# Banded attention with routed experts on one core: small tiles first, norms over more quads, the last stage's loads begun in the experts' block

## The reference

```python
xn = (x - mu) * rsqrt(var + EPS) * ln_gamma + ln_beta
abel_out = gelu(xn @ abel_w + abel_b)
topw, topi = top_k(xn @ moe_gate_w + moe_gate_b, 2); topw = softmax(topw)
h = gelu(einsum('bsd,edh->ebsh', xn, ew1) + eb1)          # 8 experts
moe_out = sum over the two chosen of (h @ ew2 + eb2) * topw
for i in range(3): moe_out = moe_out @ expm(gens[i])
gate = sigmoid(concat(abel_out, moe_out) @ gc_w + gc_b)
return x + abel_out * (1 - gate) + moe_out * gate
```

## Time and profile before

| | us |
|---|---|
| median of three timed runs | 1724.65 (1723.74 to 1725.66) |
| the profiled execution | 1724.25 |
| its span in the trace | 1722.4 |
| PE busy | 1500.2 (87%) |
| DVE busy | 1219.9 (71%) |
| ACT busy | 891.6 (52%) |
| POOL busy | 686.2 (40%) |
| DMA | 241.23 MB, 140 GB/s in the mean |

### The profile page before, as it was taken

One profiled execution on the slowest core, in us unless ns is written; L12 is line 12 of the kernel. 1 busy time (PEld: TensorE's weight loads), 2 busy tenths in 40 slices (PEclk: granted clock), 3 DMA queues, 4 the chain that ended last, 5 costly groups with the idle time before them and its releaser, 6 DMA issues. The chain is left out here.

```text
span 1722.4 us, 33082 instructions
## 1 busy us (share of the span) xinstructions
PE 1500.2 (87%) x10271; PEld 1033.1 (60%) x10272; DVE 1219.9 (71%) x3678; ACT 891.6 (52%) x1775; POOL 686.2 (40%) x698
## 2 busy tenths in 40 slices
PE   7999999999989999998999898799999999999300
PEld 5755455555545555554555466688888888888200
DVE  5667788888788788878977855456556555566197
ACT  3146766776676677667667664233333333332144
POOL 1011233533443343344244415144444444445277
PEclk9999999999999999999999999899999999999755
DMA  8132244345435434543543347655656565655397
GB/s 219 58 123 69 86 156 148 120 141 173 128 106 179 156 114 137 173 131 111 173 155 111 114 148 240 188 100 117 141 103 149 105 151 103 153 105 102 64 329 222
DMA packets 184174, 241.23 MB, mean 140 GB/s; under 512 B 23464, under 2 KB 154672, under 8 KB 183920
## 3 DMA queue, kind: packets, MB, share of 16 engines
q1 hardware_dynamic: 158464, 204.49, 37.4%
q0 software_dynamic: 25584, 35.15, 12.1%
HBM read 132.21 MB, written 104.72 MB: 138 GB/s over the span
## 5 line engine op out<-in xcount | busy, mean ns | idle before, releaser
L1116 ACT ACTIVATE pexp<-scT 128x512 f32<-128x512 f32 x768 | 436.4, 598 | 244.3 <-PE scT L882 241.9
L1322 DVE TENSOR_REDUCE mx<-work 128x1 f32<-128x320 f32 (+2 forms) x1024 | 500.3, 546 | 53.0 <-PE work L859 52.3
L1931 POOL DMA_INDIRECT y_rows<-rows_add,row_of x135 | 215.4, 1596 | 288.1 <-DMA y_rows<-rows_add,row_of 200.3
L882 PE MATMUL scT<-w 128*128 128x192 bf16 (+3 forms) x1536 | 281.1, 275 | 27.2 <-ACT pexp L1116 22.6
L859 PE MATMUL work<-w 126*128 126x320 bf16 (+4 forms) x1280 | 267.7, 295 | 25.8 <-DVE mx L1322 20.2
L1964 PE MATMUL h_ps<-inT,w1c 128*128 128x256 f32 (+1 forms) x1136 | 248.8, 373 | 4.6 <-DVE inT L2018 2.4
L1977 PE MATMUL o_ps<-w,hT 128*128 x1080 | 246.5, 381 | 5.8 <-ACT hT L1897 5.8
L1905 ACT ACTIVATE rows_add<-rows_out,row_share 128x257 f32<-128x257 f32 x135 | 61.8, 503 | 345.8 <-DVE rows_out L2036 243.9
L1964 PEld LDWEIGHTS h_ps<-inT,w1c 128*128 128x128 f32 x1136 | 210.5, 193 | 33.1 <-issue 3.1
L882 PEld LDWEIGHTS scT<-w 128*128 128x128 bf16 x1536 | 123.3, 97 | 176.3 <-ACT pexp L1116 116.3
L1977 PEld LDWEIGHTS o_ps<-w,hT 128*128 128x128 f32 x1080 | 200.3, 191 | 31.3 <-issue 6.9
(11 more groups left out here) (220 smaller groups left out, 2061.1 us busy)
## 6 DMA issues: line engine op xcount, KB each, us to landing
w<-split_spill SPq DMA_DIRECT2D x384, 128.0 KB, 2.8
split_spill<-split SPq DMA_DIRECT2D x64, 384.0 KB, 3.0
rows_in<-z_rows SPq DMA_DIRECT2D x64, 265.0 KB, 4.8
y_rows<-pre SPq DMA_DIRECT2D x16, 514.0 KB, 5.6
y<-y_rows SPq DMA_DIRECT2D x16, 514.0 KB, 6.6
x_rows<-x SPq DMA_DIRECT2D x16, 512.0 KB, 2.7
abel_rows<-pre SPq DMA_DIRECT2D x16, 512.0 KB, 3.6
abel_in<-abel_rows SPq DMA_DIRECT2D x16, 512.0 KB, 4.5
```

Source lines behind the costliest of these rows:

```text
L882: ins = nc.tensor.matmul(scT[n % 2][:, at:at + hi - lo], tile(kst[par][0:K_EXP, h, :], t), qst[par][0:K_EXP, h, lo:hi], start=True, stop=True)
L1116: nc.scalar.activation(pexp[:, (q * GROUP + n) % NPB, :], scT[n % 2][:, :], ACT.Exp, scale=DH ** -0.5).then_inc(s_exp, 1)
L1322: emptied(nc.vector.reduce_max(mx[:, c:c + 1], bank(s, "max", b, h, t)[:, 0:n], AX_X), s, "max", b, h, t)
L1931: pool.indirect_dma_start(kept.y_rows, bass.IndirectOffsetOnAxis(ap=row_of[n][:, r:r + 1], axis=0), rows_add[n % 2][:, r, :], None, comput ...
```

## The change

Four things change. (1) The eight norms of a step are done at units n = 1 and 3 of two quads each: norm_ctx in quads 4 and 5 (3 and 4 in step 16), norm_x in quads 6 and 7. (2) The order of places: place 0 has the number of the last pair (two blocks, the one that can be taken over), places 1 to 7 are the singles, places 8 to 70 are the other pairs; `tiles` writes out 12 tiles ahead of the loop instead of 4. (3) The last stage's y and base buffers are laid into w2 and w1 (5 of y, 8 of base) by the class `Tail`; SP loads base of batches 0 to 7 inside the experts' block as soon as the last w1 copy is done, and y of batches 0 to 3 when all adds have landed. (4) In the last stage a store waits only for the tile it takes; the sums of the last batch go from POOL to VectorE; a first sigmoid is done ahead of its inputs.

```diff
-LAST_NORM_CTX, LAST_STATS_AT, LAST_Z_AT = 3, 6, 10
+LAST_NORM_CTX, LAST_STATS_AT, LAST_Z_AT = (3, 4), 6, 10
-NORM_CTX, NORM_X = 5, 6
+NORM_CTX, NORM_X = (4, 5), (6, 7)
...
-    wide = np.concatenate([np.arange(NE), np.arange(NE) * region, np.arange(pairs), pairs + k // 2,
-                           np.zeros(pairs), k % 2 * P, spare]).astype(np.float32)
+    wide = np.concatenate([np.arange(NE), np.arange(NE) * region, [pairs - 1], pairs + k // 2, np.arange(pairs - 1),
+                           [0], k % 2 * P, np.zeros(pairs - 1), spare]).astype(np.float32)
...
+        self.ODDS_AT = 0
...
-                        if q == (LAST_NORM_CTX if s == B else NORM_CTX) and finish:
-                            norm_ctx(s - 2, n)
-                        if q == NORM_X and (not isinstance(s, int) or s + 1 < B):
-                            norm_x(s + 1, 1 - par, n)
+                        at = LAST_NORM_CTX if s == B else NORM_CTX
+                        if q in at and finish and n % 2:
+                            norm_ctx(s - 2, 2 * at.index(q) + n // 2)
+                        if q in NORM_X and s + 1 < B and n % 2:
+                            norm_x(s + 1, 1 - par, 2 * NORM_X.index(q) + n // 2)
...
-            no, before_last, behind = kept.pair_no, NE - 1, slice(z.PAIRS - 1, z.RTILES)
+            no, before_last, behind = kept.pair_no, NE - 1, slice(z.ODDS_AT, z.ODDS_AT + NE)
...
+class Tail:
...
+        self.YB, self.BB, self.BSEMS, self.AHEAD = 5, NE, 4, 4
...
+        self.base = [w1[:, n, :, :].rearrange("p k f -> p (k f)").rearrange("p (j d) -> p j d", d=z.D)
+                     for n in range(self.BB)]
+        self.y = [flat2[:, n * yw:(n + 1) * yw].rearrange("p (j w) -> p j w", w=z.YW) for n in range(self.YB)]
...
+    def load_base(self, sp, kept, z, b):
+        landed = self.f_early if b < self.BB else self.f_bs[b % self.BSEMS]
+        sp.dma_start(self.base[b % self.BB], kept.of_batches(kept.base_rows, z)[b]).then_inc(landed, 16)
+
+    def base_there(self, eng, b):
+        if b < self.BB:
+            eng.wait_ge(self.f_early, self.BB * 16)
+        else:
+            eng.wait_ge(self.f_bs[b % self.BSEMS], ((b - self.BB) // self.BSEMS + 1) * 16)
+
+    def load_y(self, sp, kept, z, b):
+        n = b % self.YB
+        sp.dma_start(self.y[n], kept.of_batches(kept.y_rows, z)[b]).then_inc(self.f_y[n], 16)
...
-            for t in range(4):
-                step(t, t, 0)
-            with eng.Fori(1, B - 1) as i:
+            for t in range(12):
+                step(t, t % 4, t // 4)
+            with eng.Fori(3, B - 1) as i:
...
-            return 1 if isinstance(t, int) and t >= z.PAIRS else RB
+            return 1 if isinstance(t, int) and z.ODDS_AT < t <= z.ODDS_AT + z.SINGLES else RB
...
             sp.dma_start(gcw[:, :, :], a["gcw"]).then_inc(e_gcw, 16)
+            sp.dma_start(tail.gcb[:, :], a["gcb"]).then_inc(tail.f_load, 16)
             tiles(sp, step)
             sp.wait_ge(e_bst, 16 * B)
+            sp.wait_ge(e_w1, RTILES)
+            for b in range(tail.BB):
+                tail.load_base(sp, kept, z, b)
+            sp.wait_ge(e_o, RTILES)
+            sp.wait_ge(e_added, blocks_upto(RTILES) * 16)
+            for b in range(tail.AHEAD):
+                tail.load_y(sp, kept, z, b)
...
-                sp.wait_ge(f_res, (b + 1) * NTOK)
                 for pos, blk, m in RUNS:
-                    lo = pos % 2 * BLK
-                    sp.dma_start(out[b, blk * BLK:(blk + m) * BLK, :], o[b % NB][lo:lo + m * BLK, pos // 2, :])\
+                    lo, j = pos % 2 * BLK, pos // 2
+                    if b < B - 1:
+                        sp.wait_ge(f_res, b * NTOK + j + 1)
+                    else:
+                        sp.wait_ge(f_end, j + 1)
+                    sp.dma_start(out[b, blk * BLK:(blk + m) * BLK, :], o[b % NB][lo:lo + m * BLK, j, :])\
...
-            for b in range(NB - 1):
-                load(b)
             for s in range(B + 2):
-                if s + NB - 1 < B:
-                    load(s + NB - 1)
+                if s + tail.AHEAD < B:
+                    wait(sp, f_u, (s + tail.AHEAD - YB + 1) * NTOK)
+                    tail.load_y(sp, kept, z, s + tail.AHEAD)
+                if BB <= s + tail.BSEMS - 1 < B:
+                    wait(sp, f_u, s * NTOK)
+                    tail.load_base(sp, kept, z, s + tail.BSEMS - 1)
...
             shift(B - 1)
+            for j in range(NTOK):
+                dve.wait_ge(f_o, (B - 1) * NTOK + j + 1)
+                nv.tensor_tensor(o[(B - 1) % NB][:, j, :], xs[:, B - 1, j, :], o[(B - 1) % NB][:, j, :], ALU.subtract)\
+                  .then_inc(f_end, 1)
...
-            act.wait_ge(f_load, 16)
+            act.wait_ge(tail.f_load, 16)
+            nc.scalar.activation(warm[:, :], tail.gcb[:, :], ACT.Sigmoid)
...
-            for s in range(B + 1):
-                if s < B:
-                    inverse(s)
+            for s in range(B):
+                inverse(s)
                 if s >= 1:
                     residual(s - 1)
```

More of the change, by code:

```diff
@@ L1753, in _, with __init__, sems, experts @@
                 pool.wait_ge(g_scat[i], (B // 2) * SCATTERS)
-def experts(nc, outer, a, z, kept, w1, w2, b1, b2, xs):
+class Tail:
+    def __init__(self, nc, outer, z, w1, w2):
+        def sems(name, n):
+            return [outer.enter_context(nc.semaphore(f"{name}{i}")) for i in range(n)]
+        yw = z.NTOK * z.YW
+        flat2 = w2.rearrange("p e f d -> p (e f d)")
+        self.YB, self.BB, self.BSEMS, self.AHEAD = 5, NE, 4, 4
+        assert self.YB * yw <= NE * z.FC * z.D
+        assert z.KC * z.F == z.NTOK * z.D
+        self.base = [w1[:, n, :, :].rearrange("p k f -> p (k f)").rearrange("p (j d) -> p j d", d=z.D)
+                     for n in range(self.BB)]
+        self.y = [flat2[:, n * yw:(n + 1) * yw].rearrange("p (j w) -> p j w", w=z.YW) for n in range(self.YB)]
+        self.gcb = outer.enter_context(nc.sbuf_tensor("gcb", [P, 1], F32))
+        self.f_load, = sems("f_load", 1)
+        self.f_y = sems("f_y", self.YB)
+        self.f_early, = sems("f_early", 1)
+        self.f_bs = sems("f_bs", self.BSEMS)
+    def load_base(self, sp, kept, z, b):
[9 more added lines that the diff above has]
+        sp.dma_start(self.y[n], kept.of_batches(kept.y_rows, z)[b]).then_inc(self.f_y[n], 16)
+def experts(nc, outer, a, z, kept, w1, w2, b1, b2, xs, tail):
     B, D, NTOK, KC, F, FC, RB = z.B, z.D, z.NTOK, z.KC, z.F, z.FC, z.RB
@@ L2080, in _, with last @@
             dve.wait_ge(e_adot, B)
-def last(nc, outer, a, z, kept, xs, out):
+def last(nc, outer, z, kept, xs, tail, out):
     B, D, NTOK, YW = z.B, z.D, z.NTOK, z.YW
@@ L2101, in some @@
             return [sb(f"{name}{i}", shape, dt) for i in range(NB)]
-        y = some("y", [P, NTOK, YW])
-        base = some("base", [P, NTOK, D])
+        y, base, YB, BB = tail.y, tail.base, tail.YB, tail.BB
         u = some("u", [P, NTOK, D])
@@ L2113, in last @@
         fnm = some("fnm", [P, NTOK])
-        gcb = sb("gcb", [P, 1])
-        f_load = sem("f_load")
-        f_y = [sem(f"f_y{i}") for i in range(NB)]
-        f_bs = [sem(f"f_bs{i}") for i in range(NB)]
+        warm = sb("f_warm", [P, 1])
+        f_y = tail.f_y
         f_out = [sem(f"f_out{i}") for i in range(NB)]
@@ L2175, in mixed @@
                 for j in range(NTOK):
[L2176 to L2177 removed]
+                    nv.scalar_tensor_tensor(out=u[n][:, j, :], in0=y[b % YB][:, j, 0:D], scalar=gate[n][:, j:j + 1],
+                                            in1=base[b % BB][:, j, :], op0=ALU.mult, op1=ALU.subtract).then_inc(f_u, 1)
                 for j in range(NTOK):
@@ L2201, in _ @@
             shift(B - 1)
+            for j in range(NTOK):
+                dve.wait_ge(f_o, (B - 1) * NTOK + j + 1)
+                nv.tensor_tensor(o[(B - 1) % NB][:, j, :], xs[:, B - 1, j, :], o[(B - 1) % NB][:, j, :], ALU.subtract)\
+                  .then_inc(f_end, 1)
         @block.scalar
         def _(act):
-            act.wait_ge(f_load, 16)
+            act.wait_ge(tail.f_load, 16)
+            nc.scalar.activation(warm[:, :], tail.gcb[:, :], ACT.Sigmoid)
             def gates(b):
                 act.wait_ge(f_logit, b + 1)
-                nc.scalar.activation(gate[b % NB][:, :], logit[b % NB][:, :], ACT.Sigmoid, bias=gcb[:, 0:1])\
+                nc.scalar.activation(gate[b % NB][:, :], logit[b % NB][:, :], ACT.Sigmoid, bias=tail.gcb[:, 0:1])\
                   .then_inc(f_gate, 1)
@@ L2262, in sandwich_kernel @@
         xs = weight("xs", [P, z.B, z.NTOK, z.D])
-        experts(nc, outer, a, z, kept, w1, w2, b1, b2, xs)
-        last(nc, outer, a, z, kept, xs, a["out"])
+        tail = Tail(nc, outer, z, w1, w2)
+        experts(nc, outer, a, z, kept, w1, w2, b1, b2, xs, tail)
+        last(nc, outer, z, kept, xs, tail, a["out"])
 def kernel(**inputs):
```

21 lines of the change are left out of this document (8 added, 13 removed).

## The result

The changed kernel takes 1714.6 us (median of 5 runs, 1713.8 to 1717.3) against 1724.6 us (1721.1 to 1725.7) of the kernel before beside it: ratio 0.9948, 95% interval 0.9935 to 0.9960. It is faster, by 9 us (10.0 by the medians) instead of the 19 forecast, and inside the range. The profiled execution took 1713.8 us, 1712.0 of them its span.

The account below looks back on a forecast made before the run. PE was taken to bound the front and the experts' loop, the add chain having hardly any room. Front -5, experts' block -6.5 and last stage -7.6 gave -19.1: 1724.25 to 1705.2 us, range 1690 to 1718.

Parts of the forecast that it names:

- Part 1, the front: Attention front: spreading norms over quads 4 to 7 gains 0.35 us a step, -5 us over 15 steps (bounds -21 and +9).
- PE's waits for exp would go: Front, quads 5 and 6: PE's waits for exp, 1.2 us a step, go; an xn wait of some 0.6 us appears.
- Part 2, PE's end: Experts' block: with small tiles first, PE ends at 1608.6 instead of 1614.3 us, with 6.5 us of gaps assumed.
- some 6 us of lag are free: Small tiles at the start: adds lag 5.4 us in all, within some 6 us that scale and gelu allow.
- the new tail: Block's end: two-block adds, the last landing at T + 11.9, or 1620.5 us, before the cost of the base loads.
- T: The time of PE's end in the experts' block, forecast at 1608.6 us.
- hardly any room: Experts' loop: the scatter-add chain takes 29.4 us per four tiles, the same as PE's four tiles.
- Part 3, the burst: Block's end: eight 512 KB base loads delay the adds by 3.5 us; last add lands at 1624.0, y issued at 1624.3.
- Part 4, the last stage: Last stage: first u -0.6, pace 4.69 to 4.36 us a batch -5, end -2; sum -7.6 us.
- Rival A: Front: xn wait replaces exp wait (no room at 730.90), nothing gained or up to 9 us lost; 1710 to 1719; chance 0.19.
- B: Block's end and last stage: adds stand behind the burst (+3), DMA limits the stage (5 not gained); 1713 us; chance 0.09.
- D: First small tiles: gaps keep PE's clock at 1.2 GHz, 7.5 instead of 4.4 us each; 1733 us, slower; chance 0.07.

Follow-up runs that it names:

- -7 alone: The kernel before with only the eight norms of a step spread over quads 4 to 7: 1725.0 against 1730.4 us, ratio 0.9961.
- parts 3 and 4: The changed kernel with the norms' spread and the small-tiles-first order taken back: 1723.4 us, ratio 0.9958 against the kernel before.
- part 2 alone: The kernel before with only the order of places changed, small tiles first: 1731.0 us, ratio 1.0007.
- the kernel with the loads late: The changed kernel with all eight base loads issued after the last add has landed: 1721.5 us, ratio 0.9990 against the kernel before.

## Why the prediction was half right

*Part 1, the front: right in size.* Forecast -5, 0.35 a step, with a new wait of 0.6 us a step. Measured 0.3 to 0.4 a step and -4.3 in the trace (-7 alone, -4 beside parts 3 and 4), with a wait of 4.7 / 14 = 0.34 us. That PE's waits for exp would go held only in part: over nine steps on one chip they fall from 17.7 to 10.0 us, on the other from 12.1 to 10.0.

*Part 2, PE's end: right; the adds behind it: wrong.* Forecast PE's end at 511.1 us from the first load of rows (1608.6 less 1097.5), measured 512.8 in part 2 alone. The step that failed is the pair of sentences after it: the lag was set against "some 6 us of lag are free", and the new tail was worked out from T, as if every add started on time, with its last start at T + 8.0 (a landing of 3.9 before T + 11.9). It starts at T + 15.1. The 6 us were indeed free for PE in the small tiles, where it waited for gelus 0.2 us at most. But the lag did not go away, and the same text had the row that says so: the chain needs 29.4 us for four tiles, as PE does, "hardly any room". Behind small tiles at the end there was nothing to carry it through. At the start there are over 60 tiles in which it can't be paid back. The chain was also further behind than the 5.4 us forecast, with adds 6.1 us apart instead of 4.5, partly as the bursts come twice as close together over small tiles; the text had charged them to PE alone. And it loses 5.0 us more at the loop's end, where the kernel before loses 2.3 and the sum had nothing; the cause of this part stays open. Error of this step: 8.8 us on the last add's start (527.9 instead of 519.1), 1.7 of it PE's end.

*Part 3, the burst: right in kind, too small.* Forecast +3.5. Measured 5.3 to 5.4 us on the last add (parts 3 and 4 against before; the changed kernel against part 2 alone, on another chip), and 7.4 against the kernel with the loads late. The hit interval itself has +3.7, near the 3.2 of the row taken; what the sum left out is the next interval (+1.0) and that PE, by then held by the adds, stops for 6 us in two waits. Of the rule of the Trainium skill (DMA: Bandwidth & Descriptors, "Queues, rings and completion order"), that an engine alternates between queues by packets, the runs show this much: 1.5, 2.1 and 4.2 MB beside an add cost its interval 3.2, 3.9 and 3.7 to 5.1 us, far from in proportion, as it would have it.

8.8 and 1.8 are 10.6 us; the measured error of the block is 10.3 (537.1 instead of 526.8), as the first load of y follows the last add's start 0.3 us sooner than forecast.

*Part 4, the last stage: right in kind, a little small.* Forecast 5.9 us to the first u, 4.36 a batch, -7.6 in all; measured 5.2, 4.23 and -9.9 (81.7 instead of 91.6 from the first load of y to the end). POOL is what is late next, as said: 4.19 to 4.23 us a batch in all ten traces that have part 4.

Rival A had the right doubt (the row at 730.90) at the wrong size, B had part of the burst, D's slow clock shows in a result of 5.40 us at the end, and in the small tiles in hidden matmuls of 2.99 us instead of 1.95 behind the wait of 2.15. None of them was the case that came. In the sum: 4.3 gained in the front, 3.9 lost in the block, 9.9 gained in the last stage, -10.3 in the profiled execution against -19.1.

## What to carry to other kernels

When two resources need the same time per round (here PE 29.4 us and the adds 29.4 us for four tiles), a view of busy shares names only one of them, and moving work to the front of the loop loads a lag on the other that no later round pays back. So add up the second chain over the whole block before counting on an end that it sets, and look for room in it first: here traffic cut into quarters made 1.6 us of room a round, turned a reordering worth nothing into 7 us by the traces (4.7 by the timed runs, whose intervals overlap), and gave a kernel (ratio 0.986 and 0.989 on two chips) faster than both. Beside this chain, twelve transfers of 128 KB cost less than three of 512 KB.

## What the runs showed of the hardware

- A chain of scatter-adds that each wait for the one before takes 6.55 us for two blocks. 1.5 MB of other transfers cost it 3.2 us in one piece per four tiles and 1.6 us in quarters (27.8 in the mean against 4 x 6.55 = 26.2). Which overlap brings this (a quarter may lie in the 3.1 us in which POOL issues) was not measured apart.
- 4.2 MB of loads cost an add beside them hardly more than 2.1 MB (3.7 to 5.1 and 3.9 us), though behind the last add the whole set of y and base loads, 6.3 MB, took 18.7 us from its first issue to the first u.
- What the view names as the end of a wait can be another event let go by the same one: adds at the start and the end of the block that waited for the landing before them (1135.11) are put down to ACT's scaling of the next tile (1134.36).
- The front, the same code, was up to 12 us longer in one profiled execution than in another on another chip (first load of rows at 1092.6 and, with the same part 1, at 1104.6), more than most parts of this change are worth.
